# A one-layer language-model tower on one core: GpSimd's small operations on VectorE, 64-column tiles in feed-forward and fused product, scores per head in 32-row tiles

## The reference, cut to what matters

```python
h = table[ids]                                   # 64 item + 64 geo + 24 visit features a token
item_h, geo_h, visit_h = gelu(item @ w_item + b), gelu(geo @ w_geo + b), gelu(visit @ w_visit + b)
fused = layer_norm(gelu(cat(item_h, geo_h, visit_h) @ w_fuse + b_fuse))
h = item + 0.1 * fused * valid                   # token stage
x = layernorm(h)                                 # attention, 4 heads of 16
q, k, v = x @ Wq.T + bq, x @ Wk.T + bk, x @ Wv.T + bv
h = h + bf16(softmax(q k^T / 4) v) @ Wo.T + bo
x = layernorm(h)                                 # feed-forward, routed
weights = x @ wr + br                            # the 63 largest of a sequence's 128 tokens
y = (gelu_tanh(x @ w1 + b1) @ w2 + b2) * weights # added for those 63 tokens alone
out = x + h + y (chosen tokens)
```

## Time and profile before

| | us |
|---|---|
| median of 3 runs | 580.38 (578.63 to 581.15) |
| the profiled execution | 582.28 |
| its span, first to last instruction | 580.5 |
| TensorE busy | 488.0 (84%) |
| VectorE busy | 444.6 (77%) |
| ScalarE busy | 411.6 (71%) |
| GpSimd busy | 378.0 (65%) |
| mean granted TensorE clock | 0.942 of 2.4 GHz |

### The profile page before, as it was taken

The page is one execution under the profiler, slowest core; times in us unless marked ns, Lnnn a source line. Parts: engine busy times, 40 slices in busy tenths (PEclk is TensorE's granted clock), DMA queues, the critical chain, the costliest instruction groups (busy, mean ns, idle before and its releaser), DMA issues.

```text
span 580.5 us, 14228 instructions
## 1 busy us (share of the span) xinstructions
PE 488.0 (84%) x4100; PEld 377.4 (65%) x4100; DVE 444.6 (77%) x1757; ACT 411.6 (71%) x694; POOL 378.0 (65%) x571
## 2 busy tenths in 40 slices
PE   0767788988999899898999999899998897988644
PEld 0445566767777677776777777677776765765443
DVE  5266667887888888778878888788887884887887
ACT  1326676788888788787787888788887774866730
POOL 6576456666777677667767677767776674442575
PEclk9879889999999999899999999999999997999855
DMA  3154444544454544545444444445454443333344
GB/s 99 21 94 114 100 104 82 101 105 106 108 110 109 112 106 103 111 90 112 99 95 100 106 105 109 107 107 112 112 107 99 99 100 66 90 92 91 76 102 116
DMA packets 89634, 57.74 MB, mean 99 GB/s; under 512 B 27408, under 2 KB 79248, under 8 KB 89488
## 3 DMA queue, kind: packets, MB, share of 16 engines
q1 hardware_dynamic: 83472, 47.55, 33.0%
q0 software_dynamic: 6144, 9.97, 11.8%
HBM read 11.08 MB, written 4.19 MB: 26 GB/s over the span
## 4 chain that ended last, share of the span: by engine, by line
PE 40%; ACT 16%; issue 14%; DVE 11%; POOL 9%; another core or an unknown queue 6%; DMA 2%; ACTq 0%; SPq 0%; DVEq 0%; POOLq 0%
PE psum L924 5%; POOL G L344 4%; PE psum L917 4%; PE psum L861 4%; PE psum L945 4%; ACT L520 3%; POOL rs L355 3%; PE psum L968 3%; ACT L527 3%; PE psum L943 3%; PE psum L1003 3%; PE psum L897 3%; PE psum L837 2%; PE psum L931 2%
## 5 line engine op out<-in xcount | busy, mean ns | idle before, releaser
L344 POOL DMA_INDIRECT G<-table,idx x128 | 126.6, 989 | 61.2 <-issue 58.9
L355 POOL TENSOR_TENSOR rs<-rs,minus_half 128x4 f32<-128x4 f32 x96 | 100.7, 1049 | 16.7 <-POOL rs L352 9.7
L669 DVE TENSOR_REDUCE neg_max<-psum 128x4 f32<-128x512 f32 x128 | 83.4, 674 | 0.6 <-PE psum L917 0.6
L837 PE MATMUL psum<-wt,hid 128*128 128x64 f32 x512 | 66.6, 286 | 10.1 <-ACT hid L520 10.0
L837 PEld LDWEIGHTS psum<-wt,hid 128*128 128x128 f32 x512 | 62.9, 200 | 13.4 <-ACT hid L520 13.4
L761 DVE SCALAR_TENSOR_TENSOR R<-t,rs,u 128x64 f32 (+1 forms) x128 | 52.6, 469 | 23.4 <-POOL rs L412 23.4
L352 POOL TENSOR_SCALAR rs<-mv 128x4 f32<-128x4 f32 x96 | 22.9, 238 | 72.7 <-DVE mv L580 69.0
L527 ACT ACTIVATE prob<-psum 128x512 f32<-128x512 f32 x128 | 69.7, 613 | 0.5 <-PE psum L880 0.2
L585 DVE TENSOR_SCALAR x<-R,mv,rs 128x64 f32 (+1 forms) x256 | 62.5, 308 | 4.8 <-POOL rs L355 4.8
L520 ACT ACTIVATE hid<-psum,wt 128x512 f32<-128x512 f32 x64 | 40.5, 684 | 29.7 <-remote 19.8
L724 DVE SCALAR_TENSOR_TENSOR q_s<-psum,wt,q_mask 128x512 fp32r<-128x512 f32 x32 | 24.0, 751 | 41.9 <-ACT q_mask L498 24.4
(11 more groups left out here) (116 smaller groups left out, 1138.8 us busy)
## 6 DMA issues: line engine op xcount, KB each, us to landing
q_bd<-q_s SPq DMA_DIRECT2D x256, 64.0 KB
k_bd<-k_hi SPq DMA_DIRECT2D x128, 64.0 KB
k_pair<-k_hi SPq DMA_DIRECT2D x64, 128.0 KB
k_pair<-k_lo SPq DMA_DIRECT2D x64, 128.0 KB
out<-R SPq DMA_DIRECT2D x11, 256.0 KB, 3.0
G<-table,idx POOLq DMA_INDIRECT x128
wt<-packed SPq DMA_DIRECT2D x1, 1028.5 KB, 5.4
out<-R SPq DMA_DIRECT2D x2, 512.0 KB, 4.0
```

Of the source, the lines that this page charges most:

```text
L344: pool.indirect_dma_start(G[par][:, b, :], None, table, bass.IndirectOffsetOnAxis(ap=idx[par][:, b:b + 1], axis=0),).then_inc(gathered[par ...
L355: pool.tensor_tensor(rs[:, :], rs[:, :], minus_half[:, :], ALU.pow).then_inc(S[dst], 1)
L669: dve.tensor_reduce(neg_max[:, HEADS * s:HEADS * s + HEADS], bank[SCORES[s]][:, :].rearrange("p (h k) -> p h k", h=HEADS), AX, ALU.max, ne ...
L837: last = mm(bank[ffn_bank(d) + 1][:, s * D:(s + 1) * D], hid[:, m, slot(s)[0]], w["w_2"][:, m * D:(m + 1) * D], start=(m == 0), stop=(m == 1))
```

## The change

It moves to VectorE the index copy, the additions of epsilon (new tiles `ve1` to `ve3`) and the multiplication by `valid` (new tile `rm1`); GpSimd keeps the power. `w_fe` and `w_fo` become one 64-column `w_f`, in two column tiles. `ffn_second` has w2 as the stationary operand in 64-column tiles and 256 moving columns; y comes out transposed, ScalarE copies it with its bias (`ffn_copy`), TensorE transposes it back (`ffn_back`), and VectorE copies it to `Y`. A bank of scores now holds one head of the four sequences. Both kinds of scores are made by 32-row tiles straight from `q_s`, `k_hi` and `k_lo`: the first kind by 16 matmuls of 128 columns, the second by 4 of 512 (`shifts`) and 32 of 128. SyncE's 16 DMAs a step at L287, L295, L304 and L311, their tiles and the clearing of these (L563, L564) are gone; the DMA of the maxima stays and writes 4 rows. `q_s` has two buffers.

```diff
@@ sync
-                    wait(sp, "s_ready", GB, b - 1)
-                    for h in range(HEADS):
-                        rows = slice(32 * h, 32 * h + 32)
-                        sp.dma_start(k_bd[rows, :, h, :].bitcast(F32),
...
-                                         ).then_inc(q_bd_in[1 - odd], 16)
...
-                                     k_lo[1 - odd][rows, :].bitcast(F32)
-                                     ).then_inc(k_pair_in[1 - odd], 16)
@@ gpsimd
-                pool.tensor_copy(idx[par][:, :], of(idx_all, g)).then_inc(S["idx_ready"], 1)
...
-                pool.tensor_scalar(rs[:, :], mv[:, :, 1], LN_EPS, None, ALU.add
-                                   ).then_inc(S[dst], 1)
-                wait(pool, dst, 2, g, 1, alone=True)
-                pool.tensor_tensor(rs[:, :], rs[:, :], minus_half[:, :], ALU.pow
+                pool.tensor_tensor(rs[:, :], ve[:, :], minus_half[:, :], ALU.pow
                                    ).then_inc(S[dst], 1)
...
-                    pool.tensor_tensor(rs1[:, :], rs1[:, :], of(valid, a), ALU.mult
-                                       ).then_inc(S["rm1_ready"], 1)
@@ scalar
+            def ffn_copy(d):
+                wait(act, "f2_ready", 1, d)
+                ends(act, "yb_ready", 1, d - 1)
+                act.activation(y_t[:, :], bank[ffn_bank(d) + 1][:, 0:2 * P], ACT.Identity,
+                               bias=w["b_2"]).then_inc(S["yt_ready"], 1)
...
-                for s in range(GB):
+                for h in range(HEADS):
                     if on(c):
                         ends(act, "pv_ready", 1, c - 1)
-                        wait(act, "st_ready", GB, c, s + 1)
+                        wait(act, "st_ready", HEADS, c, h + 1)
...
-                    if s == 0 and on(e) and not late(i):
+                    if h == 0 and on(e) and not late(i):
                         attention_out(e)
+                    if h == 1 and on(d) and not late(i):
+                        ffn_copy(d)
@@ vector
+                wait(dve, mv_done, 1, g)
+                dve.tensor_scalar(ve[:, :], mv[:, :, 1], LN_EPS, None, ALU.add
+                                  ).then_inc(S[ve_done], 1)
...
-                wait(dve, "f2_ready", 1, d)
-                dve.tensor_tensor(
+                wait(dve, "yb_ready", 1, d)
+                dve.tensor_copy(
...
-                    w["b2"].unsqueeze(1).to_broadcast([P, GB, D]), ALU.add
...
+                if on(i + 3):
+                    dve.tensor_copy(idx[1 - odd][:, :], of(idx_all, i + 3)
+                                    ).then_inc(S["idx_ready"], 1)
...
-                    wait(dve, "rm1_ready", 1, a)
+                    wait(dve, "rs1_ready", 1, a, alone=True)
+                    dve.tensor_tensor(rm1[:, :], rs1[:, :], of(valid, a), ALU.mult
+                                      ).then_inc(S["rm1_ready"], 1)
+                    wait(dve, "rm1_ready", 1, a, alone=True)
@@ tensor
-                for s in range(GB):
-                    for m in range(2):
-                        last = mm(bank[ffn_bank(d) + 1][:, s * D:(s + 1) * D],
-                                  hid[:, m, slot(s)[0]], w["w_2"][:, m * D:(m + 1) * D],
-                                  start=(m == 0), stop=(m == 1))
+                for m in range(2):
+                    for r in range(2):
+                        last = mm(bank[ffn_bank(d) + 1][r * D:(r + 1) * D, 0:2 * P],
+                                  w["w_2"][:, m * D:(m + 1) * D],
+                                  hid[:, m, r * 2 * P:(r + 1) * 2 * P],
+                                  start=(m == 0), stop=(m == 1), tile_position=(0, r * D))
...
+            def ffn_back(d):
+                wait(pe, "yt_ready", 1, d)
+                for j in range(2):
+                    last = mm(bank[ffn_bank(d) + 1][:, j * P:(j + 1) * P],
+                              y_t[:, j * P:(j + 1) * P], ident, start=True, stop=True,
+                              is_transpose=True)
+                last.then_inc(S["yb_ready"], 1)
...
+            def shifts():
+                for h in range(HEADS):
+                    rows = slice(ROW * h, ROW * h + ROW)
+                    mm(bank[h][:, :], ones_r[rows, :], max_row[rows, :], start=True, stop=False,
+                       tile_position=(ROW * h, 0))
+            def scores_t(odd, at):
+                tok = slice(at * P, (at + 1) * P)
+                for part in (k_hi, k_lo):
+                    for h in range(HEADS):
+                        rows = slice(ROW * h, ROW * h + ROW)
+                        last = mm(bank[h][:, tok], part[odd][rows, tok], q_s[odd][rows, tok],
...
-                    for s in range(GB):
-                        wait(pe, "prob_ready", GB, c - 1, s + 1)
-                        tok, at = slot(s)
-                        mm(bank[SCORES[s]][:, :], q_s[:, tok],
-                           k_bd[:, at, :, :].rearrange("p h k -> p (h k)"), start=True, stop=True
+                    wait(pe, "prob_ready", HEADS, c - 1)
+                    for at in range(GB):
+                        tok = slice(at * P, (at + 1) * P)
+                        for h in range(HEADS):
+                            rows = slice(ROW * h, ROW * h + ROW)
+                            last = mm(bank[h][:, tok], q_s[odd][rows, tok], k_hi[odd][rows, tok],
...
-                    for n, wf in enumerate(("w_fe", "w_fo")):
-                        last = mm(bank[6][:, 0:2 * P], w[wf],
+                    for n in range(2):
+                        last = mm(bank[6][n * D:(n + 1) * D, 0:2 * P], w["w_f"],
...
                     wait(pe, "max_row_in", 16, c)
-                    pe.wait_ge(q_bd_in[odd], half * 128 + 128)
-                    pe.wait_ge(k_pair_in[odd], half * 64 + 64)
-                    scores_t(c, odd, (0,))
                     wait(pe, "qs_ready", 1, c + 1)
-                    scores_t(c, odd, (1,))
...
                     wait(pe, "kl_ready", 1, c + 1)
-                    scores_t(c, odd, (2,))
+                    shifts()
+                    for at in range(GB):
...
                 if on(d) and not late(i):
                     ffn_second(d)
                 if on(e) and not late(i):
                     project(e)
+                if on(d) and not late(i):
+                    ffn_back(d)
```

More of the change, by code:

```diff
@@ L125, in build @@
         q_mask = sb("q_mask", [P, GT])
-        q_s = sb("q_s", [P, GT], F32R)
-        q_bd = [sb(f"q_bd{p}", [P, GB, 2, 2, P], F32R) for p in range(2)]
-        k_pair = [sb(f"k_pair{p}", [P, 2, GT], F32R) for p in range(2)]
-        k_bd = sb("k_bd", [P, GB, HEADS, P], F32R)
+        q_s = [sb(f"q_s{p}", [P, GT], F32R) for p in range(2)]
         k_hi = [sb(f"k_hi{p}", [P, GT], F32R) for p in range(2)]
@@ L409, in step @@
                 if on(a):
[L410 to L413 removed]
+                    rstd(ve1, rs1, "ve1_ready", "rs1_ready", a)
                 if on(d):
@@ L510, in step @@
                     wait(act, "k_ready", 2, b)
-                    if on(b - 2):
-                        act.wait_ge(k_pair_in[1 - odd], (half + odd) * 64)
-                    ends(act, "k_bd_in", 64, b - 2)
+                    ends(act, "st_ready", HEADS, b - 2)
                     act.activation(by_row(k_hi[1 - odd][:, :]), two_banks(K_BANKS), ACT.Identity,
                                    bias=w["b_k"]).then_inc(S["kh_ready"], 1)
+                if type(i) is int and i == NG + 1:
+                    ffn_copy(NG - 2)
                 if on(d):
@@ L561, in _ @@
             dve.tensor_copy(wo_part[:, 2, :], wo_rest[:, 1, :]).then_inc(consts_ready, 1)
-            for tile in q_bd:
-                dve.memset(tile[:, :, :, :, :].bitcast(F32), 0.0)
-            dve.memset(k_bd[:, :, :, :].bitcast(F32), 0.0).then_inc(bd_zeros_ready, 1)
             setup_steps = 4
@@ L694, in step @@
                 if on(b):
-                    wait(dve, "rs2_ready", 2, b)
+                    wait(dve, "rs2_ready", 1, b)
                     ends(dve, "xt_ready", 1, b - 1)
@@ L703, in step @@
                 if on(d):
-                    wait(dve, "rs3_ready", 2, d)
+                    wait(dve, "rs3_ready", 1, d)
                     ends(dve, "r_ready", 1, d - 1)
@@ L738, in step @@
                 if on(a):
-                    moments(st1, mv1, "st1_ready", "mv1_ready", a)
-                    wait(dve, "mv1_ready", 1, a)
+                    moments(st1, mv1, ve1, "st1_ready", "mv1_ready", "ve1_ready", a)
                     for s in range(GB):
@@ L784, in step @@
                     add_routed(3)
-            pipeline(dve, step)
+            pipeline(dve, step, ahead=3)
             take_weights(1)
@@ L872, in values_back @@
                 last.then_inc(S["pb_ready"], 1)
-            def scores_t(c, odd, seqs):
-                for s in seqs:
-                    tok, at = slot(s)
-                    mm(bank[SCORES[s]][:, :], ones_r[:, :], max_row[:, s, :], start=True, stop=False)
-                    for pair in range(2):
```

(19 more changed lines are left out.)

128 lines of the change are left out of this document (49 added, 79 removed).

## The result

The changed kernel takes 666.4 us (median of 4 runs, 656.5 to 671.5) against 580.8 for the kernel before (4 runs): ratio 1.137, interval 1.123 to 1.151. Forecast were 563. The profiled execution of after is the longest of the four, 671.5 us with a span of 669.6. A second comparison of the same pair, on another chip, gave 668.4 against 585.3, ratio 1.143 (1.130 to 1.157).

A forecast was written before the change was run, and what follows sets the result against it. No single engine bounds it: TensorE and ScalarE hand the step to each other, plus late semaphores. From 582.3 us, 22 steps at -0.48 and start, jam and tail terms total -17.2: 565.1, less 1.9 for the median, 563; range 548 to 592.

The forecast's parts named there:

- Copies gone: SyncE loses 16 DMAs a step, and ScalarE's late-semaphore waits go with them: -0.93 us a step, bounds 0 and -0.93.
- The prediction's own sign of being wrong: Remote waits of over 10 us in all staying on ScalarE, or VectorE having no idle time left.
- Rival 1: Gathers alone delay semaphores, so those waits stay and the new feed-forward chain adds on top: 596 us, chance 0.14.
- The ffn line: TensorE's feed-forward passes shrink from 1.8 to 2.0 us to 0.85 + 0.2; gain off the path, way back on it.
- First scores: On TensorE, 16 row-tile matmuls, four at a time: 0.43 us plus about 0.2 for the block; upper bound 1.8.
- second scores: On TensorE, 4 spreads and 8 groups of four take 1.3 us, hidden up to 2.5; upper bound 4.5.
- ffn_copy: ScalarE gets this copy at 0.38 us, bounds 0.38 and 0.47, delaying the last exponential by 0.35.
- VectorE's small jobs: Index copy, three additions and one multiplication cost VectorE 1.1 us a step, bounds 0.8 and 2.0.
- Rival 3: VectorE becomes the bound at 0.4 us per small job: 15.5 to 15.6 us a step, 578 us, chance 0.14.
- The new round: Step period through `Y`, the maxima and the exponentials: 15.1 us, 0.48 below the mean step before.
- Rival 4: Feed-forward way back hidden in slack at the maxima: 14.6 us a step, 549 us, chance 0.17.
- Rival 2: TensorE's tile loads run one after another, scores come late: 17.5 us a step, about 635 us, chance 0.05.

The follow-up runs named there:

- table of four: Changed kernel with its gathers 666 us; with two filling matmuls added 589; with plain loads instead of gathers 601; with both 563.
- e9: Changed kernel with plain loads in place of every gather and two filling matmuls before `project`: 563.0 us, ratio 1.006 to the kernel before.
- e10: Changed kernel with ScalarE's copy `o_t` ahead of the four exponentials instead of behind the first: 619.6 us, ratio 1.105 to the kernel before.
- e12: Kernel before with the small operations on VectorE and the new scores, feed-forward and fused products as before: 563.4 us, ratio 1.002.
- e4: Changed kernel with GpSimd issuing a step's four gathers only when that step's values product has ended: 621.5 us, ratio 1.067 to the kernel before.
- e2: Kernel before with only the scores changed (32-row tiles, no copies, two `q_s` buffers): 615.7 us, ratio 1.052.

## Why the prediction was wrong

- **Copies gone**, the failed step. It read the late semaphores as "gathers and copies together", and took -0.93 us a step for the copies' going. The 16 copies went, and the sum of the late increments is 169 us where it was 165; with plain loads and no gathers it is 0. So the copies are not needed for the hold and the gathers are. The prediction's own sign of being wrong, over 10 us of "remote" waits on ScalarE, came with 56.1 us before `pv_t` alone. Its evidence against (no such wait in the first 45 us) was true and misread: after, without any copies, has none there either, so what is missing in the first 45 us is something else, and no run shows what.
- **Rival 1** had the condition right (more than half of the 0.93 remains) and the price wrong, 596 against 666. It kept the hold where it was. But the change moved the values into the gathers, where ScalarE now stands still for up to 3.5 us a step behind a late increment. That and the next point have to make up the 70 us between 596 and 666; the table of four tells them apart only in part.
- **The clock**, the second failed step, left out of every term and every rival. Each part was costed at 2.4 GHz, and a shorter product was "hidden" at zero cost. The ffn line says that the gain "is not on the path". That it uncovers a wait of 1.1 to 1.3 us for `o_t`, and what the clock does behind such a standstill, was in no step. Two filling matmuls are worth 77 us. The trace of before had it to be read: its clock falls five times in the first 245 us, at 243.2 us behind standstills of 1.24 and 0.40 us (there are others as long with no fall behind them).
- **First scores** 0.67 us (0.43 and 0.2 forecast); **second scores** 314.27 to 315.55, 1.28 us (1.3); **fused product** 0.58 us in e9 (0.63); **ffn_second** 1.08 us (1.05); **ffn_back** 0.44 (0.38). Right. Four 32-row tiles run side by side: in L867 a group of four starts every 0.11 us, where 107 ns were assumed. The Trainium skill ("TensorE: Matmul & The Clock Gate", Part 3) lets a load overlap matmuls in flight when its row group is another one, and the trace agrees, now for four row groups.
- **ffn_copy** 0.49 us, above both bounds (0.38, 0.47).
- **VectorE's small jobs** (+1.1): the index copy takes 0.16 us, each of the three additions 0.18 and the multiplication 0.47, together 1.16 a step. Right in sum. Rival 3 is out: where nothing else disturbs (e9), VectorE is busy 81% and the step is 15.14 us, not 15.5.
- **The new round**, 15.1 us. Right, where its two silent conditions hold: e9, without late increments and with the clock held, takes 15.14 us a step (14.92 and 15.36 in turn, which the forecast didn't have). In after it is 18.6. Rival 4, which wants 14.6, is out by the same steps.
- **Rival 2** (loads one after another) is out by the 0.67 us.

## What to carry to other kernels

Before shortening work on TensorE, list the waits that this work covers. Where one is laid bare or lengthened, look in the clock row for what the clock did behind such standstills already; the lower clock can cost several times what the edit saves. No length of a standstill decides it here: the clock fell behind some of 0.4 us and stayed up behind others of 1.3 us. An engine's filler, or a slower form of a product that keeps it at work, can be the faster kernel. A wait named "remote" is best tested by removing one suspect at a time before a forecast is built on it, and a part that gains alone has to be tested in the company in which it is to run.

## What was not expected of the hardware

- TensorE's semaphore increments come up to 3.1 us late in after, and 3.8 in before, while GpSimd issues indirect gathers; of the other engines no such one is found, as far as their events are recorded; and plain loads of the same bytes from SyncE leave them on time (0 of 1,028). On one of the experiments' five chips none was late with gathers either (e10 to e12).
- The clock settled into a pattern with the steps: in e4 it was 27.3 us at 2.4 GHz and 6.8 us at 1.2 GHz over and over, two steps (14.9 and 19.2 us) long, with the fall behind every second step's standstill.
- Open: why the hold is on some chips only, why it spares the first 45 us, and what in an indirect gather causes it; and what makes the clock fall in the kernel with the scores alone (e2). Not tried: gathers in another form or spread over the step.
